# A gated cross-attention and mixture-of-experts block: pitch of the rows sent to the experts, and four steps that are moved

## The reference, cut to what matters

```python
x = x + tanh(g_xattn) * attention(layernorm(x), ctx, ctx, group_prob, mask)   # 16 batches, 112 rows, 375 keys, 16 heads of 16
n = layernorm(x); n = n * rsqrt(mean(n**2) + 1e-8) * norm_weight               # 1,792 tokens of 256
shared = relu(n @ sw1 + sb1) @ sw2 + sb2                                       # 256 -> 1024 -> 256
scores, idx = top_k(sigmoid(n @ router_w.T), 2)                                # 2 of 8 experts
w = scores / (sum(scores) + 1e-6)
routed = sum over the two of w_e * (relu(n @ ew1[e] + eb1[e]) @ ew2[e] + eb2[e])
x = x + tanh(g_ffn) * (shared + routed)
```

## Time and profile before

| What | Value |
|---|---|
| Runs | 658.57, 659.84, 664.95 us |
| Profiled execution | 662.9 us, of which the span of the program's instructions is 661.1 us |
| TensorE busy | 583.0 us (88%), 6,006 matmuls |
| VectorE busy | 435.1 us (66%) |
| ScalarE busy | 429.8 us (65%) |
| GpSimd busy | 311.7 us (47%) |
| Mean granted TensorE clock | 0.944 of 2.4 GHz |
| DRAM traffic | 84.29 MB by DMA packets, mean 127 GB/s |

### The profile page before, as it was taken

One profiled execution on the slowest core, in us unless ns is written; L12 is line 12 of the kernel. 1 busy time (PEld: TensorE's weight loads), 2 busy tenths in 40 slices (PEclk: granted clock), 3 DMA queues, 4 the chain that ended last, 5 costly groups with the idle time before them and its releaser, 6 DMA issues.

```text
span 661.1 us, 18993 instructions
## 1 busy us (share of the span) xinstructions
PE 583.0 (88%) x6006; PEld 490.9 (74%) x6006; DVE 435.1 (66%) x1182; ACT 429.8 (65%) x1071; POOL 311.7 (47%) x357
## 2 busy tenths in 40 slices
PE   2679999999999999999958894799999999999950
PEld 2347888888888888888747781588888888888840
DVE  5957888888888888888985651245555536536327
ACT  4367888888888888888847531347565656656330
POOL 8303655544444447763360177143476555558120
PEclk9898999999999999999986896799999999999995
DMA  8724657776565566734110042021544643552228
GB/s 230 177 72 104 171 138 192 207 201 151 144 150 150 149 151 154 166 93 138 63 64 2 12 149 104 24 79 38 155 151 120 193 119 104 129 159 56 57 71 311
DMA packets 106777, 84.29 MB, mean 127 GB/s; under 512 B 42915, under 2 KB 100517, under 8 KB 106606
## 3 DMA queue, kind: packets, MB, share of 16 engines
q1 hardware_dynamic: 103694, 75.59, 43.5%
q0 software_dynamic: 3040, 8.16, 3.4%
HBM read 50.45 MB, written 28.30 MB: 119 GB/s over the span
## 4 chain that ended last, share of the span: by engine, by line
PE 61%; issue 8%; ACT 6%; DVE 6%; POOL 5%; DMA 4%; SPq 1%; POOLq 0%; ACTq 0%; DVEq 0%
PE ps L1204 15%; PE ps L1177 14%; PE ps L1028 10%; PE ps L1046 5%; PE ps L945 5%; PE ps L1015 5%; PE ps L976 4%; ACT probs L804 3%; POOL w L661 2%; ACT ctxT L728 2%; DMA probs<-x_sent 2%; POOL w L659 2%; DVE probs L1351 1%; DVE x_sb L1588 1%; PE ps L1170 1%
## 5 line engine op out<-in xcount | busy, mean ns | idle before, releaser
L1028 PE MATMUL ps<-ident,probs 112*125 112x112 f32 x768 | 193.1, 277 | 1.1 <-ACT arena L795 0.5
L804 ACT ACTIVATE probs<-probs,negmax 112x375 f32<-112x375 f32 x256 | 154.4, 606 | 12.6 <-DVE negmax L1351 12.1
L863 ACT ACTIVATE arena<-ps,b 128x256 f32<-128x256 f32 x192 | 79.5, 464 | 123.2 <-PE ps L1177 108.9
L1028 PEld LDWEIGHTS ps<-ident,probs 112*125 112x125 f32 x768 | 139.5, 188 | 22.4 <-issue 9.2
L1204 PE MATMUL ps<-w,arena 128*128 128x256 f16 x1152 | 136.6, 278 | 12.1 <-issue 10.7
L1351 DVE CUSTOM_DVE_ANT_0 probs<-ps,neg 112x375 f32<-112x375 f32 x256 | 136.8, 540 | 5.0 <-issue 1.3
L1520 DVE TENSOR_TENSOR arena<-arena 128x512 f16<-128x512 f32 x96 | 74.6, 785 | 96.1 <-ACT arena L868 86.8
L1204 PEld LDWEIGHTS ps<-w,arena 128*128 128x128 f16 x1152 | 113.7, 99 | 31.5 <-issue 16.2
L1363 DVE TENSOR_TENSOR arena<-ps,gpT 125x336 f32<-125x336 f32 x192 | 97.1, 506 | 39.8 <-PE ps L1028 35.9
L561 POOL TENSOR_TENSOR probs<-probs,gp_in 112x375 f32<-112x375 f32 x64 | 58.7, 917 | 133.2 <-ACT probs L804 132.6
L1177 PE MATMUL ps<-probs,w 128*128 x816 | 92.1, 273 | 1.0 <-issue 0.4
(11 more groups left out here) (176 smaller groups left out, 800.8 us busy)
## 6 DMA issues: line engine op xcount, KB each, us to landing
kst<-k_scratch SPq DMA_DIRECT2D x64, 140.6 KB, 3.7
w1s<-in_L_ffn_ew_dram SPq DMA_DIRECT2D x8, 1024.0 KB
w2s<-in_L_ffn_ew_dram SPq DMA_DIRECT2D x8, 1024.0 KB, 5.7
x_sent<-y_sb SPq DMA_DIRECT2D x12, 516.0 KB, 6.0
ctx_in<-in_ctx_dram SPq DMA_DIRECT2D x16, 375.0 KB
k_scratch<-kT SPq DMA_DIRECT2D x32, 187.5 KB, 2.5
arena<-y_back SPq DMA_DIRECT2D x7, 512.0 KB, 6.9
k_scratch<-kT SPq DMA_DIRECT2D x32, 93.8 KB, 2.0
```

The costliest lines, as they stand in the source:

```text
L804: act.activation(probs[:, n % PROBS], probs[:, n % PROBS], ACT.Exp, bias=negmax[:, p, n:n + 1], scale=-1.0, accum_out=rowsum[:, p, ORDER[n ...
L863: act.activation(hid32[:, f], ps[:, f // 2 % 4, f % 2 * TILE:(f % 2 + 1) * TILE], ACT.Relu, bias=b1[:, f, e:e + 1]).then_inc(h_relu, 1)
L1028: mm = pe.transpose(ps[0:KP, PT[n % 2], c * S:(c + 1) * S], probs[:, n % PROBS, c * KP:(c + 1) * KP], ident[0:S, 0:S])
```

## The change

Six edits come together.

1. A row of `x_sent` has 544 float16, 1,088 bytes, instead of 516 (a multiple of 32 float16). The two words stay behind the 512 halves, and 28 float16 of padding follow. `xpair` in SBUF gets the same pitch, and with it the tile qT becomes wider: 14 x 544 = 7,616 columns instead of 7,224. The padding is sent and zeroed too. The loads of the words read 4 float16 of a row, as before.
2. POOL clears the columns of qT behind the queries, once at the start, and PE's first product of values waits for that too (`ctx_pad` 2).
3. ACT copies the second half of the turned context after the exponential of head 0, not of head 1.
4. POOL spreads the last inverse sums after the first three products by norm_weight, not ahead of them.
5. DVE does the splits of tile 0 of the shared expert first, then the choice of experts, then the addition of tile 0, the splits of tile 1, place_pairs and the addition of tile 1.
6. PE does results of tile 0 and hidden of tile 1 ahead of rank_pairs, then results of tile 1. Its loop covers tiles 2 to 5.

```diff
--- before.py
+++ after.py
@@ -28,7 +28,9 @@
 ZT = -(-(RT + 2) // ZEROS)
 ROWS = ZT * ZEROS * TILE
 assert ROWS >= (RT + 2) * TILE
-RW = 2 * D + 4
+WORDS = 4
+LINE = 32
+RW = -(-(2 * D + WORDS) // LINE) * LINE
 YPAD = 4
 YROWS = YPAD + 2 * T
 SMALLS = 10
@@ -148,7 +150,7 @@
         est_i = sb("est_i", [P, 2, E], I32)
         tile_of = sb("tile_of", [P, E + 2], I32)
         token_row = sb("token_row", [P, NT], I32)
-        words_in = sb("words_in", [P, TILE // P, RW - 2 * D], F16)
+        words_in = sb("words_in", [P, TILE // P, WORDS], F16)
         words = words_in[:, :, :].bitcast(F32)
         dest = sb("dest", [P, TILE // P], I32)
         slots = sb("slots", [P, 2, NT], I32)
@@ -438,7 +440,7 @@
                                        x_sent[bass.ds(r * TILE, TILE), 0:2 * D]).then_inc(xT_in, 16)
 
             def load_words(r):
-                sp.dma_start(words_in[:, :, :], x_sent[bass.ds(r * TILE, TILE), 2 * D:RW].rearrange("(a p) c -> p a c", p=P)).then_inc(words_sent, 16)
+                sp.dma_start(words_in[:, :, :], x_sent[bass.ds(r * TILE, TILE), 2 * D:2 * D + WORDS].rearrange("(a p) c -> p a c", p=P)).then_inc(words_sent, 16)
 
             sp.wait_ge(scattered, 16 * 2 * NT)
             load_turned(0)
@@ -501,6 +503,7 @@
             pool.wait_ge(gap_zero, 1)
             pool.memset(qb_words, 0.0).then_inc(gap_zero, 1)
             pool.memset(ctxT[:, :, :, S2:S2P], 0.0).then_inc(ctx_pad, 1)
+            pool.memset(qT_all[:, 2 * ND * T:], 0.0).then_inc(ctx_pad, 1)
             pool.memset(bv_rows[:, :], 0.0).then_inc(bias_rows, 1)
             pool.memset(bv_ones[:, :], 0.0).then_inc(bias_rows, 1)
             pool.wait_ge(bias_rows, 2)
@@ -648,7 +651,6 @@
                 step(t, t % 2, t // 2 + 1, (t + 1) // 2 + 1)
             step(B - 2, 0, B // 2, B // 2, more=False)
             step(B - 1, 1, B // 2, None, more=False, last=True)
-            spread_inverse(B - 1)
 
 
             def split_down(n, p):
@@ -662,6 +664,8 @@
 
             pool.wait_ge(in_small, 16 * SMALLS)
             for i in range(NT):
+                if i == 3:
+                    spread_inverse(B - 1)
                 if i == 2 * (H - PJ_FROM) - 2:
                     split_out(B - 1)
                 pool.wait_ge(n2_centered, i + 1)
@@ -807,7 +811,7 @@
                         copy_probs(t, n - LEAD + 1)
                     if n == LEAD - 2:
                         prep_piece(t + 1, GP, 1 - p)
-                    if t_next and not first and n == LEAD - 3:
+                    if t_next and not first and n == LEAD - 4:
                         prep_piece(t + 1, CTX1, 1 - p)
                     if t_next and n in PIECES:
                         prep_piece(t + 1, PIECES[n], 1 - p)
@@ -966,7 +970,7 @@
                         pe.wait_ge(prep_lo, 2 * b + 1)
                         if isinstance(b, int) and b == 0:
                             pe.wait_ge(w_lo, 5)
-                            pe.wait_ge(ctx_pad, 1)
+                            pe.wait_ge(ctx_pad, 2)
                     elif c == 0:
                         pe.wait_ge(prep_lo, 2 * b + 2)
                 to = ps[:, prep_bank(p, VALUES2 if c == 2 else VALUES01), c % 2 * D:c % 2 * D + D]
@@ -1219,10 +1223,12 @@
                 pe.matmul(rk, ones16[:, :], count16[:, 1].rearrange("p i e -> p (i e)"), start=False, stop=True).then_inc(rank_mm, 1)
                 pe.matmul(ps[:, PR[1], NT * E:(NT + 1) * E], ones16[:, :], count16[:, 2, 0], start=True, stop=True).then_inc(rank_mm, 1)
 
-            rank_pairs()
             pe.wait_ge(w2_lo, 1)
             results(0, 0)
-            with pe.Fori(1, ST - 1) as i:
+            hidden(0, shared_rows(1))
+            rank_pairs()
+            results(1, 0)
+            with pe.Fori(2, ST - 1) as i:
                 shared_tile(i)
             shared_tile(ST - 1)
             pe.wait_ge(tiles_made, 1)
@@ -1461,8 +1467,6 @@
                 normal_low(2 * j + 1)
 
 
-            dve.wait_ge(rl_mm, NT)
-            dve.wait_ge(sum_zero, E + 3)
             logit = ps[:, PR[1], P:P + NT * E].rearrange("p (i e) -> p i e", e=E)
 
             def spread(col):
@@ -1482,16 +1486,20 @@
                     src, to = buf(k % 2), buf((k + 1) % 2)
                     then(dve.tensor_tensor(to[:, pad:pad + n], src[:, pad:pad + n], src[:, pad - 2 ** k:pad - 2 ** k + n], ALU.add))
 
-            choose(logit, 0)
-            then(dve.scalar_tensor_tensor(rt[:, 2], rt[:, 0], -BIG, logit, ALU.mult, ALU.add))
-            choose(rt[:, 2], 1)
-            then(dve.tensor_tensor(before[:, 0, NTP:NTP + NT], rt[:, 0], rt[:, 1], ALU.add))
-            then(dve.tensor_copy(count16[:, 0], before[:, 0, NTP:NTP + NT]))
-
-            running(lambda k: before[:, k], NT, NTP, 4)
-            then(dve.tensor_copy(count16[:, 1], before[:, 0, NTP - 1:NTP - 1 + NT]))
-            dve.tensor_copy(count16[:, 2, 0], before[:, 0, NTP + NT - 1]).then_inc(cnt_made, 1)
-            dve.tensor_copy(xwords[:, :, 1], top[:, 2]).then_inc(word_made, 1)
+            def choose_experts():
+
+                dve.wait_ge(rl_mm, NT)
+                dve.wait_ge(sum_zero, E + 3)
+                choose(logit, 0)
+                then(dve.scalar_tensor_tensor(rt[:, 2], rt[:, 0], -BIG, logit, ALU.mult, ALU.add))
+                choose(rt[:, 2], 1)
+                then(dve.tensor_tensor(before[:, 0, NTP:NTP + NT], rt[:, 0], rt[:, 1], ALU.add))
+                then(dve.tensor_copy(count16[:, 0], before[:, 0, NTP:NTP + NT]))
+
+                running(lambda k: before[:, k], NT, NTP, 4)
+                then(dve.tensor_copy(count16[:, 1], before[:, 0, NTP - 1:NTP - 1 + NT]))
+                dve.tensor_copy(count16[:, 2, 0], before[:, 0, NTP + NT - 1]).then_inc(cnt_made, 1)
+                dve.tensor_copy(xwords[:, :, 1], top[:, 2]).then_inc(word_made, 1)
 
             def place_pairs():
 
@@ -1524,9 +1532,8 @@
                 dve.wait_ge(w1_hi, n + 1)
                 dve.tensor_tensor(w1[:, p, LO], w1s[:, :, :], w1[:, p, HI], ALU.subtract).then_inc(w1_lo, 1)
 
-            def shared_tile(i):
-
-                split_hidden(i)
+            def add_shared(i):
+
                 two = bass.ds(2 * i, 2)
                 dve.tensor_tensor(x_sb[:, two], x_sb[:, two], sb2_bc[:, :].unsqueeze(1).to_broadcast([P, 2, D]), ALU.add).then_inc(sb2_added, 1)
                 dve.wait_ge(sb2_added, i + 1)
@@ -1548,14 +1555,19 @@
                 then(dve.tensor_tensor(top[:, 6:8], top[:, 6:8], top[:, 9].unsqueeze(1).to_broadcast([P, 2, NT]), ALU.mult))
 
             then(dve.tensor_scalar(sb2_bc[:, :], sb2_bc[:, :], gates[:, 1:2], None, ALU.mult))
-            shared_tile(0)
+            split_hidden(0)
+            choose_experts()
+            add_shared(0)
+            split_hidden(1)
             place_pairs()
-            shared_tile(1)
+            add_shared(1)
             split_up_low(1, 1)
-            shared_tile(2)
+            split_hidden(2)
+            add_shared(2)
             weigh_pairs()
             with dve.Fori(3, ST) as i:
-                shared_tile(i)
+                split_hidden(i)
+                add_shared(i)
 
             dve.wait_ge(z_done, 16 * ZEROS)
             dve.wait_ge(in_b2, 16)
```

## The result

| | before | after |
|---|---|---|
| median of 8 and 8 runs | 661.48 us (658.16 to 664.95) | 656.02 us (654.76 to 658.16) |
| ratio, 95% interval | | 0.9928 [0.9901, 0.9954] |
| profiled execution, its span | 662.9, 661.1 us | 655.12, 653.3 us |

The change takes off 5.5 us, 0.8%. Forecast were 9.0 us, on the assumption that the stall of TensorE in the shared expert keeps its length. It did not: tile 3 takes 6.6 us longer than before, which is about half of what had been gained ahead of it.

The account below looks back on a forecast made before the run. The prediction took TensorE to bound the kernel. Its terms, -4.5 (context copy), -0.7 (inverse sums) and -3.8 (choice of experts), summed to -9.0 us: from 659.84 to 650.8 us as a median, 653.9 profiled; range 642 to 662.

Parts of the forecast that it names:

- the stall: Shared expert, tile 3: matmuls come one by one while GpSimd scatters rows; 30.2 us instead of 10.5, a cost of 19.7.
- Context copy: Attention loop: copying one head earlier removes all 14 waits of TensorE, -4.5 us; bounds 0 and -4.5.
- Inverse sums: Ahead of the routing: spreading them after three products lets split_out start earlier, -0.7 us; bounds 0 and -2.1.
- Choice of experts: Shared expert, tile 0: results start right behind hidden at full clock, -3.8 us; bounds 0 and -4.1.
- Scatter 3.2 us later on the old scale: GpSimd's scatter: starts 3.2 us later since place_pairs waits for tile 1's splits; covered unless the stall hangs on it.
- Pitch and clearing: Scatter rows of 1,088 bytes: 0, bounds -19.7 and +2.1; clearing qT's tail at the start: 0, bound +0.4 us.
- A, the forecast: the stall keeps its length: Shared expert: the stall begins 22 us after the first scatter DMA, ends 3 after the last; 650.8 us, chance 0.48.
- B: Shared expert: the stall begins at VectorE's loop entry, ends with the scatter, lasts 29.3 us; -2.0, 657.8 us, chance 0.26.
- Rival C: Shared expert: the stall goes, with the aligned pitch or the code's new place; 632 us, 641 to 645 if shrunk, chance 0.15.
- Rival D: Scatter: wider rows lengthen each of 28 DMAs by d and TensorE hangs on its end; -2.0 + 28d, chance 0.11.

Follow-up runs that it names:

- p1: Kernel before with only the copy of the turned context's second half moved after head 0's exponential, chip without the stall: 635.8 against 643.19 us, ratio 0.9896.
- c2: Kernel before with only the spreading of the last inverse sums put behind three of the norm's casts, chip with the stall: 662.07 against 661.8 us.
- p3: Kernel before with only rows of 1,088 bytes and the cleared tail of qT, chip without the stall: 644.08 us, ratio 1.0013.
- p2: Kernel before with only the new order of the choice of experts on VectorE and TensorE, chip without the stall: 639.7 us, ratio 0.9947.
- c4: Changed kernel with TensorE's, ScalarE's and VectorE's loops over the shared tiles written out, chip with the stall: 656.78 us (one run).
- p4: Changed kernel with rows at 1,032 bytes again, the three moves kept, chip without the stall: 632.37 us, ratio 0.9829.

## Why the prediction missed

**Context copy: the mechanism was right, the size was not.** The forecast took 4.5 us, from TensorE's matmuls that waited for the copy, and called that the upper bound. p1 gave 6.7 us, with an interval that just reaches down to 4.3; the traces are clearer. The last copy stands at 294.9 to 296.6 in the four profiles with the copy in its old place (mean 295.53), and at 287.6 to 290.7 in the sixteen with it one head earlier (mean 288.87): 6.7 us again, so that 2 of the 8.7 us in the table above are the spread of single executions. The right row was beside the one that I used. In the kernel before, the same question also says what the weight loads of the same line waited:

```profile
who waited for it (us, times):
  PEld ps L945: 7.0, 14
  PE ps L945: 4.5, 14
```

The weight loads' 7.0 us is near what was gained. That the matmuls' idle time is too short because the ends of matmuls are modelled in a profile is my reading, not shown.

**Inverse sums:** forecast 0.7; the stretch from the last copy to the first transpose shrank by 0.6 us here and by 0.75 in c2. Right.

**Choice of experts:** forecast 3.8 up to the start of tile 1. From the first transpose to there it took 372.09 - 345.28 = 26.81 us before and 358.81 - 335.99 = 22.82 after: 4.0. Right. From there to tile 3 another 1.1 us went: TensorE had waited 0.85 us for the splits of tile 2 (388.82 above). That wait belongs to the first lateness of the stall and not to the order of the code: the splits waited for ScalarE's late pair, and p1 and p3, with the old order on a chip without the stall, have no such wait (in p3 results of tile 2 start 5.24 us behind their hidden layer). On the chips with the stall both are lost; on the other p2 got 3.4 us, with a new wait of 1.1 us for the turned tokens.

**Scatter 3.2 us later on the old scale:** from the last copy to the first scatter DMA 80.1 us before and 82.6 after, and with the 0.6 of the inverse sums that is 3.1. Right, and here it counted.

**Pitch and clearing:** forecast 0; p3 has 1.0013. Right. The Trainium skill (DMA: Bandwidth & Descriptors, How a descriptor splits into AXI transactions) says that the bytes before an unaligned start cost beats. By it neither pitch is aligned and no gain was due, and the means of 1089 and 1088 ns agree.

**The failed step is "A, the forecast: the stall keeps its length".** I let the stall begin 22 us after the first scatter DMA, as in the kernel before (398.53 - 376.71 = 21.8), so that it would keep its length of 19.7 us over tile 3's own 10.5. But TensorE's starts broke up in tile 3 again, 384.37 - 370.52 = 13.9 us after the first scatter DMA, and the end came with the scatter, so tile 3 lost 36.7 - 10.5 = 26.2 us. So it was B's outcome, priced at 657.8 where 656.0 was measured, but not by B's reason in full: its end is as B has it, while its start is not VectorE's entry into the loop. The crawl shows at 384.37, VectorE's last step before the loop ends at 385.28, and c4 has no loop.

With the measured terms in B's sum it comes out near the result; that is an account after the fact and no test. Time ends with the scatter, so only what moves the scatter counts: -6.7 (copy) - 0.6 (inverse sums) + 3.1 (slots later) and the scatter itself, 37.55 us from its first start to its last end instead of 38.69, -1.1. Together -5.3 us; the medians say -5.5. The 5.0 us that TensorE saves between the transposes and tile 3 (4.0 by the reordering, 1.1 by the early lateness) are lost in the stall.

**Rival C** (632) priced the kernel without the stall well: on a chip without it the changed kernel with the old pitch takes 632.4 us. But the change does not remove the stall, and its reasons were wrong: p1, p2 and p3 have no stall there either, with the old pitch in two of them and the old place of the code in two. The rule of the Trainium skill that the prediction weighed there (Runtime: NRT & Kernel Launch, Instruction fetch mechanics), that a taken branch to code not yet loaded forces a fetch, is no explanation: c4 has no loop in these tiles and has the stall, and no load of code falls in its crawl. The prediction's case against C, that the same scatter ran beside two full tiles without harm, does not hold either: the second of them gave its first pair 2.4 us late. **Rival D** is out: the DMAs' mean is 1047 ns. Its test, p3, has 1089 against 1088 with the order unchanged.

Against the forecast's -9.0 this is 2.2 more for the copy and 5.8 less for the rest: 3.8 of TensorE's gain that the stall took, 3.1 of the slots' delay, and 1.1 back for the shorter scatter. The range held the time.

## What to carry to other kernels

When a stretch ends at a fixed distance behind another engine's work, it is that engine's start that counts: a gain ahead of it on the waiting engine is worth nothing, and a delay of the other is paid in full. To date such a stretch, look at the engines that read the results, and not at the waiting engine's own starts alone. Read a wait on TensorE by its weight loads as well as by its matmuls. And look at the kernel before on more than one chip before putting a price on an unexplained wait: here its largest one, 20 us, appeared on some chips only.

## What was not expected of the hardware

- **One program, two times.** The kernel before takes 658 to 665 us on some chips and 639 to 645 us on others. No chip showed both, but only chip 13 was used at two times, so the chip is the likely reason and not a proven one. On the first kind tile 3 takes 29 to 38 us, on the second 10.5 in every profile, p3 among them, which differs from before in the pitch alone.
- **TensorE's records run ahead of its results in the stall.** In the kernel after, ScalarE gets its first pair, the product of 12 matmuls, at 389.37, when the timeline already shows 43 matmuls of the tile as started, and its second, after 24, at 399.91, when it shows 55: about 31 ahead. Without a stall ScalarE is 1.5 us behind the start of the tile (p4), some 14 matmuls of 0.11 us, 2 ahead. So the crawl seen from 384.37 began for the results before the tile's start, over 4 us earlier than its first single matmul: the results of tile 2, which VectorE has at 379.60 in p4, just before tile 3's start at 379.66, came at 381.61 and 382.96. That is why 31 to 39 matmuls stand in front of it in every profile, loop or no loop: that count is depth of a queue, as I read it, and no place in the program.
- In the crawl the starts lie on a grid of about 0.7 us (in the rows of tile 3 above 394.98, 395.68, 396.38, 397.10, then 1.4 apart), at clock 0.5, while GpSimd's DMAs keep their pace of 1.27 us. What holds TensorE there, no run showed.
